# The key-query diagonal of a chunked delta rule in sixteen 32-token products per chunk instead of eight 64-token ones

## What is computed

```python
q = _l2norm(einsum(x, Wq)); k = _l2norm(einsum(x, Wk)); v = einsum(x, Wv)
q, k, v = (silu(causal_depthwise_conv(t, 4 taps)) for t in (q, k, v))
beta = sigmoid(einsum(x, Wb)); g = -exp(A_log) * softplus(einsum(x, Wfa, Wfb) + dt_bias)
def step(Sst, inp):                       # once per token, per batch and head
    qt, kt, vt, gt, bt = inp
    Sst = Sst * exp(gt)[..., :, None]
    err = vt - einsum('bhk,bhkv->bhv', kt, Sst)
    Sst = Sst + bt[..., None, None] * kt[..., :, None] * err[..., None, :]
    return Sst, einsum('bhk,bhkv->bhv', qt, Sst)
out = (rms_norm(attn) * sigmoid(gate)) @ Wo
```

## Time and profile before

| what | value |
|---|---|
| median of 3 runs | 983.42 us (980.95 to 990.35) |
| span of the profiled execution | 975.1 us |
| PE busy in it | 891.2 us (91%) |
| VectorE (DVE) busy | 796.5 us (82%) |
| ScalarE (ACT) busy | 708.4 us (73%) |
| weight loads (PEld) | 642.9 us, 24490 of them |
| chain that ended last | PE 83%, DVE 7%, issue 4%, ACT 4% |

### The profile page before, as it was taken

One profiled execution on the slowest core, in us unless ns is written; L12 is line 12 of the kernel. 1 busy time (PEld: TensorE's weight loads), 2 busy tenths in 40 slices (PEclk: granted clock), 3 DMA queues, 4 the chain that ended last, 5 costly groups with the idle time before them and its releaser, 6 DMA issues.

```text
span 975.1 us, 53508 instructions
## 1 busy us (share of the span) xinstructions
PE 891.2 (91%) x24490; PEld 642.9 (66%) x24490; DVE 796.5 (82%) x1612; ACT 708.4 (73%) x1780; POOL 133.7 (14%) x307
## 2 busy tenths in 40 slices
PE   4889699999999999999999999899999998878886
PEld 4534356666677767777777667677776677667775
DVE  5577879888899989999999888799889999666424
ACT  3377758788888778888888788788878887555341
POOL 7000101111111101111111110111101111111000
PEclk9999889999999999999999999999999999998879
DMA  6100111100000111200001112000000000000001
GB/s 161 60 1 9 36 33 34 44 15 15 15 4 3 34 34 34 83 8 15 15 4 34 34 33 75 16 15 15 14 15 14 14 16 15 15 4 4 3 2 44
DMA packets 29110, 25.37 MB, mean 26 GB/s; under 512 B 4626, under 2 KB 24276, under 8 KB 28884
## 3 DMA queue, kind: packets, MB, share of 16 engines
q1 hardware_dynamic: 28884, 21.94, 8.1%
HBM read 20.82 MB, written 1.11 MB: 22 GB/s over the span
## 4 chain that ended last, share of the span: by engine, by line
PE 83%; DVE 7%; issue 4%; ACT 4%; POOL 2%; POOLq 0%; DVEq 0%; ACTq 0%
PE psum L893 17%; PE psum L951 13%; PE psum L926 6%; PE psum L1037 6%; PE psum L899 4%; PE psum L1015 3%; PE psum L1009 3%; PE psum L1002 3%; PE psum L988 3%; PE psum L995 3%; PE psum L908 3%; PE psum L903 3%; PE psum L933 2%; PE psum L962 2%; PE psum L978 2%
## 5 line engine op out<-in xcount | busy, mean ns | idle before, releaser
L893 PE MATMUL psum<-hT,gw 128*128 128x512 f32 x384 | 189.0, 618 | 0.8 <-ACT hT L554 0.8
L1332 DVE SCALAR_TENSOR_TENSOR qkv<-pad,chan,qkv 128x512 f32<-128x512 f32 x192 | 141.4, 776 | 0.1
L893 PEld LDWEIGHTS psum<-hT,gw 128*128 128x128 f32 x384 | 72.7, 196 | 89.3 <-issue 86.8
L1358 DVE TENSOR_TENSOR kq<-kq,tot 128x512 f32<-128x512 f32 x160 | 110.5, 691 | 22.8 <-PE psum L926 22.7
L1376 DVE COPY_PREDICATED pairs<-masks,psum 128x256 f32<-128x256 uint8 x192 | 101.8, 530 | 23.3 <-PE psum L926 14.1
L615 ACT ACTIVATE tmat<-psum 128x128 f32<-128x128 f32 x128 | 35.8, 280 | 94.1 <-PE psum L951 93.9
L951 PEld LDWEIGHTS psum<-fmat,pairs 32*32 32x32 f32 x4096 | 46.6, 107 | 60.8 <-issue 54.2
L623 ACT ACTIVATE rr<-rl 64x512 f32<-64x512 f32 x128 | 80.3, 627 | 1.7
L926 PE MATMUL psum<-kq,ks 128*32 128x32 f32 x5120 | 76.4, 200 | 2.5 <-issue 1.6
L610 ACT ACT_TABLE_LOAD x58 | 74.4, 1283 | 1.0
L1337 DVE SCALAR_TENSOR_TENSOR qkv<-pad,chan,qkv 128x512 f32<-128x512 f32 x96 | 72.2, 752 | 3.3 <-ACT qkv L655 3.3
(11 more groups left out here) (172 smaller groups left out, 1959.9 us busy)
## 6 DMA issues: line engine op xcount, KB each, us to landing
bb<-beta_rows SPq DMA_DIRECT2D x32, 256.0 KB, 3.4
gw<-in_L_attn_Wq SPq DMA_DIRECT2D x16, 128.0 KB, 2.3
gw<-in_L_attn_Wk SPq DMA_DIRECT2D x16, 128.0 KB, 2.4
gw<-in_L_attn_Wv SPq DMA_DIRECT2D x16, 128.0 KB, 2.3
gwo<-in_L_attn_Wo SPq DMA_DIRECT2D x4, 512.0 KB, 5.8
x<-in_L_attn_hidden_states SPq DMA_DIRECT2D x4, 256.0 KB, 4.4
gfb<-in_L_attn_Wfb SPq DMA_DIRECT2D x16, 64.0 KB, 2.2
ggb<-in_L_attn_Wgb SPq DMA_DIRECT2D x4, 256.0 KB, 5.0
```

The costliest lines, as they stand in the source:

```text
L893: last = eng.matmul(two(bank[to]), gw[:, t, kt, hh * D:(hh + 1) * D], two(hT[:, kt])[:, :, h * PW:(h + 1) * PW], start=(kt == 0), stop=(kt ...
L1332: last = eng.scalar_tensor_tensor(out=piece(t, i), in0=src, scalar=tap_weight(t, tap, i), in1=piece(t, i), op0=ALU.mult, op1=ALU.add)
L1358: eng.tensor_tensor(half(kq[:, p], h, 1), half(kq[:, p], h, 1), lower.rearrange("p (a n o) -> p a n o", a=1, o=1).broadcast_to((P, 2, nb, ...
```

## The change

The diagonal of each head and batch is computed in two blocks of 32 tokens, each into its own 32-column tile of the array and its own 32x32 block of the bank. The 32x32 blocks off the diagonal are no longer computed; the bank keeps what it held there, and the mask multiplies it by zero. Nothing else is touched: the place in the order, the semaphore on the last product and VectorE's reader are the same.

```diff
             def diagonal(p):
                 for u in range(G):
                     for b in range(B):
-                        last = eng.matmul(cell(bank[DG_BANK][:, 0:UC], b, u), ks[:, p, tokens(b, u)],
-                                          kraw[:, 1, tokens(b, u)], start=True, stop=True)
+                        for j in range(2):
+                            at = slice(u * P + b * C + j * QUARTER, u * P + b * C + (j + 1) * QUARTER)
+                            last = eng.matmul(block_of(bank[DG_BANK][:, 0:UC], b, u, j), ks[:, p, at],
+                                              kraw[:, 1, at], start=True, stop=True)
                 return last
```

## The result

The changed kernel takes 1010.8 us in the median of 4 runs against 986.3 for the kernel before beside it, 24.5 us more. Forecast were 995 (+1.2%) with an upper end of 1003. The direction was right, the size was not: the loss is over twice the 12 us of the forecast.

The account below looks back on a forecast made before the run. The prediction took PE's instruction stream, with stops where fetched packets end, to bound the kernel. Supply +14 and own stream -2.3 made +11.7 on 983.4, so 995 us (+1.2%), with a range of 982 to 1003.

Parts of the forecast that it names:

- What bounds PE, and the stops: Whole span: PE's chain sets the time; PE stops inside blocks where fetched packets of 256 instructions end.
- the shift by 12 pairs: Packet ends in each slot: the boundary moves 12 pairs earlier each slot, not 4 later, leaving the cheap places.
- The own stream: Diagonal block on PE: 0.39 us for 0.46, -0.07 us a slot, -2.3 us over 32 slots.
- The supply: Instruction fetch in the dense small products: four more packets, more and longer stops, +14 us.
- the turn of 3.3 us: Time from one packet's first instruction to the next's, fitted to before: stops of 39 us become 52, +13.
- rival 1: Stops at packet ends: the places average out, +7.4 - 2.3 = +5 us, 988; chance 0.23.
- longer turns or with read-ahead: Stops at packet ends: a turn of 3.73 us gives +17; PE's sequencer reading 32 to 48 instructions ahead gives +16 to +20.
- a stop may lead PE's clock to fall for a while: PE's clock behind supply stops: possible extra loss, given no size, left out of the sum and in the range.
- Rival 3: Diagonal block: small products cost as much as wider ones, 29 ns a pair, +14.7 us, 998; chance 0.02.
- rival 2: Instruction fetch: supply has slack, stops stay at 39 us, narrower tiles decide, 981; chance 0.12.
- Rival 4: Instruction fetch: worse supply, or packets delayed beside bulk transfers, +19 us or more, over 1002; chance 0.08.
- a stop might be hidden in the last stage: Last sixth of the span: part of a stop may hide where PE would wait for VectorE anyway; left out of the sum.

Follow-up runs that it names:

- half_diag: Changed kernel without the second 32 tokens of each block of 64 in the diagonal, at the kernel before's instruction count; ratio 1.004 to the kernel before.
- wide0: Kernel before with the level 0 products as eight products of 64 tokens, 16 pairs a slot fewer; ratio 0.993.
- shift32: Kernel before with 16 extra products of 32 columns (64 instructions) once, ahead of the first diagonal; ratio 1.020.
- after_again: The changed kernel measured once more, unchanged, against the kernel before; ratio 1.033.
- wide_all: Kernel before with the products of all levels below the last as eight products of 64 tokens each, 80 pairs a slot fewer; ratio 1.001.
- gap_long: Kernel before with PE waiting for a GpSimd power operation ahead of project_output in 16 slots, gaps of 1.5 us in the mean; ratio 1.024.
- gap_short: Kernel before with PE waiting for a GpSimd addition ahead of project_output in 16 slots, gaps of 0.6 us in the mean; ratio 1.009.

## Why the prediction was right and wrong

- **What bounds PE, and the stops.** Right. The packets of 256 instructions, the stop at their end, the shift by 12 pairs (30, 18, 6 above), the four packets more and the 25002 loads are each as written.
- **The own stream, -2.3 us.** Right: 0.39 for 0.46 a slot. The floor of about 25 ns from start to start that the Trainium skill gives (TensorE: Matmul & The Clock Gate, "Wait — 56ns, not 53.3ns?") did not show: 32 pairs took 0.39 us, 12 ns each. In half_diag, on two column tiles, it was 23 ns a pair (0.37 / 16).
- **The supply, +14 us.** Right in size: +13.0 in the waits. It was the turn of 3.3 us fitted to before, with the places counted slot by slot, that gave +13; the average over all places (+7.4, rival 1) was too low, and the sums with longer turns or with read-ahead (+16 to +20) too high. That the fit met the size is in part luck: it was made to 39 us of stops in before, which the later count puts at 30 to 37, and the same method was too high for wide0. That places matter, the heart of the argument against rival 1, is shown by shift32. The Trainium skill (Runtime: NRT & Kernel Launch, "Instruction fetch mechanics") describes refills in such blocks of 256 and calls the cost of their boundary "mostly hidden"; issue waits of 38.3 and 27.5 us in spans of 1004.8 and 975.1 do not agree.
- **"... a stop may lead PE's clock to fall for a while. I leave both out of the sum and in the range."** This is the step that failed: a term put at nothing. It is +17 us in the profile of 1004.8 us and +27 us in the mean of the executions of after_again, more than the supply itself. It is about the whole miss: 11.7 and 17 make 29, where that profile's span is 27.8 us over the mean of before. The rows to see it were there: the page's PEclk row (tenths of the granted clock in 40 slices; first before, then changed), and the stop of 1.9 us on L1002, which ends at 355.65 in before and has the half clock right behind it, as its only one between 145 and 870 us:

```profile
PEclk9999889999999999999999999999999999998879
PEclk9899799999999999999999999999999997878889
```

```profile
355.90:359.30 3.40, 3.40 (x11) 2.56 (x9) 0.65 (x1) 3.03 (x4) 0.00 (x0) 0.50 0.02 5
```

A stop of 1.7 us was counted at 1.7; with a fall it costs some 3.4. A term that comes at the places of one in the sum and has its sign belongs in the sum, if only as its count times a chance: the changed kernel had 11 gaps of over 1.5 us where before had 6. The upper end of 1003 was then too low for the same reason. What feeds the term is shown in part. shift32 has as many more waits as the changed kernel (+14.5) and a clock term of 10 us, so the stops account for some 10. half_diag has 10 us of it without more waits, and the changed kernel's falls are more frequent at equal gaps; the cause of that part stays open.
- **Rival 3** (small products cost as much as the wider) and **rival 2** (the supply has slack) are excluded by the 0.39 us and by the waits. Rival 4, worse supply, had a time near the measured one by another mechanism than the one that made it. A rival in which the narrow products let the clock fall was not in the prediction, and it is the one that the runs leave standing for a part.
- That a stop might be hidden in the last stage played no visible part: the sum of the three terms leaves under 2 us.

## What to carry to other kernels

When a PE stream of many small products has stops inside blocks, released by nothing, count the instructions of one loop turn against the packet size seen on the instruction queue: the stop's drift from turn to turn tells whether it is supply. Then the price of an edit is not only its work but how many instructions it puts into the densest stretch and where it moves the packet ends; a wide product placed inside the burst gave the fetch time here at a price of 4 to 8 us of PE's stream. And price each long stop together with the clock behind it, from the clocks of many executions rather than of one profile.

## What the runs showed of the hardware

- One packet of 16 KB holds 256 PE instructions: two for each load-product pair and 272 others of PE, divided by 256, give 192.4, 196.4, 188.4 and 172.4 for before, changed, wide0 and wide_all, and the queue shows 192, 196, 188 and 172. The least time from entering one packet to entering the next is 3.73 us at the one stop where it was read the earlier trace rows, of which the transfer is 1.23; 3.3 us is an estimate, fitted to the stops of before. 128 pairs of the burst need some 2 us (2.50 / 160 each).
- 64 more instructions at one place made a kernel of 49,000 PE instructions 2% slower (1.011 to 1.029, shift32).
- The granted clock falls from 2.4 to 1.2 GHz at some gaps of an otherwise full stream, for one or more stretches of 3.4 us: at 5 of the 16 gaps of 1.5 us that gap_long makes and one of the 16 of 0.6 us of gap_short, at 45 of 53 gaps over 1.5 us in the six profiles of before and changed and at 9 of 129 from 0.3 to 0.8 us. Eight products of 128x256 then took 3.75 us instead of 1.97.
- Sixteen pairs of 128x32 on two of the four column tiles took 0.37 us, thirty-two on all four 0.39; a block of 64 columns took 0.62 us in front of one of 32 columns and 0.46 in front of its like.
